# A network of six blocks on one core: context attention reordered, recurrent prologue with composite weights on four row groups

## The reference

```python
# block 1: cross attention, 16 heads of 8, padding mask over 512 keys
q = _ln((x @ Wq.T + bq).reshape(b, s1, h, d), qn_w, qn_b) * scale
k = _ln(k, kn_w, kn_b)
attn = jnp.where(padding_mask[:, None, None, :], einsum('bihd,bjhd->bhij', q, k), -inf)
ctx = einsum('bhij,bjhd->bihd', softmax(attn, axis=-1), v)
out = ctx @ Wo.T + bo
# blocks 2 and 3: self attention with a window, mixture of experts
# block 4: recurrent, 32 steps, with attention over the context in each
gates = concat([x_t, attn]) @ W_ih.T + b_ih + h @ W_hh.T + b_hh
i, f, g, o = split(gates, 4)
c = sigmoid(f) * c + sigmoid(i) * tanh(g);  h = sigmoid(o) * tanh(c)
attn = attend(h)
# block 5: four state space layers, in each
dt = (u @ xpw)[..., :DT_RANK]           # DT_RANK = 8
delta = softplus(dt @ dtw + dtb)
# block 6: experts with low-rank additions
```

## Time and profile before

| | us |
|---|---|
| median of 3 runs | 657.27 |
| lowest, highest run | 653.38, 658.79 |
| the profiled execution | 659.21 |
| its span (first to last instruction) | 657.1 |

### The profile page before, as it was taken

How to read it: one execution, slowest core, us unless ns; L and a number is a source line. 1 busy time by engine, 2 the same in 40 slices (tenths; PEclk the granted TensorE clock), 3 DMA queues, 4 the chain that set the end, 5 groups by cost and what they waited for, 6 DMA issues and landing times.

```text
span 657.1 us, 20737 instructions
## 1 busy us (share of the span) xinstructions
PE 557.8 (85%) x8469; PEld 426.5 (65%) x8469; DVE 470.8 (72%) x1829; ACT 311.0 (47%) x910; POOL 167.3 (25%) x209
## 2 busy tenths in 40 slices
PE   6968769769997999999999999966998898889847
PEld 4635545368875888888888888854655664666435
DVE  2867639865345777777777777752888998998882
ACT  2768729226556334444443444335545554554501
POOL 4245624127000000000000000005357346644700
PEclk9969979599995555555555555557988998999896
DMA  8900000010002000000000000000000000000000
GB/s 317 421 8 2 1 5 1 2 47 1 1 6 90 4 4 3 5 4 3 4 5 3 4 3 5 4 2 0 1 0 2 0 1 1 0 1 0 1 0 8
DMA packets 6255, 16.05 MB, mean 24 GB/s; under 512 B 2656, under 2 KB 3432, under 8 KB 5648
## 3 DMA queue, kind: packets, MB, share of 16 engines
q1 hardware_dynamic: 5744, 14.47, 6.0%
q10 hardware_dynamic: 416, 0.26, 0.1%
HBM read 14.60 MB, written 0.13 MB: 22 GB/s over the span
## 4 chain that ended last, share of the span: by engine, by line
PE 42%; DVE 31%; ACT 14%; issue 10%; POOL 2%; DMA 1%; DVEq 0%; ACTq 0%
PE bank L1715 7%; PE bank L1621 6%; PE bank L1783 6%; ACT esp L671 3%; PE bank L1551 3%; PE bank L1564 2%; DVE ssum L1164 2%; ACT a L658 2%; ACT e L673 2%; DVE w L1219 2%; DVE rz L1199 2%; DVE opre L1140 2%; DVE asp L1154 2%; DVE opre L1143 2%; DVE opre L1141 2%
## 5 line engine op out<-in xcount | busy, mean ns | idle before, releaser
L1621 PE MATMUL bank<-esp,qblk 128*128 128x1 f16 (+1 forms) x2048 | 66.6, 166 | 11.9 <-ACT esp L671 11.9
L1621 PEld LDWEIGHTS bank<-esp,qblk 128*128 128x128 f16 x2048 | 61.2, 104 | 17.3 <-ACT esp L671 17.3
L470 POOL MEMSET ctxT<- 128x128 f32 x1 | 0.3, 316 | 277.6 <-DVE xres L1206 277.6
L1621 PE MATMUL bank<-hsp,kT 128*128 128x2 f16 x2048 | 63.5, 166 | 2.0 <-DVE hsp L1192 1.9
L1621 PEld LDWEIGHTS bank<-hsp,kT 128*128 128x128 f16 x2048 | 59.5, 104 | 2.2 <-issue 2.2
L658 ACT ACTIVATE a<-opre 128x4 f32<-128x4 f32 x64 | 13.1, 205 | 80.6 <-DVE opre L1143 80.6
L1232 DVE SCALAR_TENSOR_TENSOR T<-bank,bct,T 128x256 f32<-128x256 f32 x112 | 46.4, 473 | 2.2 <-PE bank L1796 2.2
L1219 DVE TENSOR_TENSOR_SCAN qblk<-ctxT,bank 128x512 f32<-128x512 f32 x32 | 37.7, 1209 | 5.7 <-PE bank L1783 5.3
L665 ACT ACTIVATE gact<-bank,lgate 128x16 f32<-128x16 f32 x64 | 17.6, 275 | 46.4 <-PE bank L1621 46.4
L1219 DVE TENSOR_TENSOR_SCAN w<-kT,bank 128x512 f32<-128x512 f32 x32 | 37.6, 1206 | 1.1 <-PE bank L1783 1.1
L1783 PE MATMUL bank<-maskb,T 128*128 128x512 f32 x64 | 37.4, 712 | 0.5 <-ACT T L743 0.5
(11 more groups left out here) (326 smaller groups left out, 1403.7 us busy)
## 6 DMA issues: line engine op xcount, KB each, us to landing
w<-in_w_dram SPq DMA_DIRECT2D x2, 2048.0 KB
ctxT<-in_ctxT_dram SPq DMA_DIRECT2D x8, 256.0 KB, 6.2
wqkv<-in_qkvT_dram SPq DMA_DIRECT2D x1, 1536.0 KB, 12.1
w<-in_mw_dram SPq DMA_DIRECT2D x1, 1024.0 KB, 5.1
lw<-in_lw_dram SPq DMA_DIRECT2D x1, 960.0 KB, 25.0
rows<-in_rows_dram SPq DMA_DIRECT2D x1, 772.0 KB, 9.5
wqkv<-in_fw_dram SPq DMA_DIRECT2D x1, 532.0 KB, 3.5
T<-in_mask_dram SPq DMA_DIRECT2D x1, 512.0 KB, 6.0
```

Of the source, the lines that this page charges most:

```text
L1621: return pe.matmul(out, lhsT, rhs, start=start, stop=stop, skip_group_check=True)
```

## The change

In the context attention the instructions stay and their order changes on three engines. PE runs the scores one batch earlier, between the third and the fourth transpose of a batch, and each of the four now waits for one maximum; the values of a batch come after the transposes of the next. VectorE takes the reciprocal two groups behind the maximum and not one, and the copy and `x_heads` at other places. ScalarE runs up to five exponentials ahead of the copies.

In the recurrent prologue ScalarE writes only `gx32`; GpSimd makes the bfloat16 high part from it. The 8-row operands of the composite weights lie on four row groups (partitions 0, 32, 64 and 96), one for each layer, and the layers take turns. For this the transposes become matmuls with the identity, onto four groups of output partitions, with 32 columns of which 8 are meant; `dtw` is loaded by four DMAs; four copies to `xpd` take the place of two. ScalarE, not VectorE, copies the four products to `wdt`, after its table load. The semaphores `l_gxps` and `m_comp` become one, `l_ps`.

```diff
@@ -239,10 +239,10 @@
         m_out = lw[:, 0:ML * MC * D]
-        m_dt = maskb[:, :].bitcast(F32)[:, 0:ML * MC * MR]
+        m_dt = maskb[:, :].bitcast(F32)[:, 0:ML * MC * MR + 32]
         diagc = vx[:, :, :].rearrange("p n d -> p (n d)")
-        dtw = maskb[0:MR, :].bitcast(F32)[:, 1024:1024 + ML * MI]
-        xpd = wqkv[0:MR, 1856:1856 + ML * MI]
+        dtw = [maskb[32 * l:32 * l + MR, :].bitcast(F32)[:, 1024:1024 + MI] for l in range(ML)]
+        xpd = [wqkv[32 * l:32 * l + MR, 1856:1856 + MI] for l in range(ML)]
         biasT = sb("m_biasT", [2 * ML * MC, P])
@@ -287,11 +287,11 @@
              "f_gate", "f_sub", "f_exp", "f_cw", "f_cwps", "f_cwT", "f_h", "f_act", "f_y", "f_acc", "f_b2")
-        sems("d_lw", "l_w", "l_stat", "l_max", "l_scale", "l_kv", "l_hi", "l_rest", "l_gxps", "l_gx",
+        sems("d_lw", "l_w", "l_stat", "l_max", "l_scale", "l_kv", "l_hi", "l_rest", "l_ps", "l_gx", "l_gxhigh",
              "l_gxlow", "l_zero", "g_ps", "g_act", "c_new", "c_tanh", "h_hi", "h_lo", "s_hi", "m_c", "m_t", "m_d",
...
              "y_st", "y_tr")
-        sems("d_late", "d_ssm", "m_turns", "m_comp", "m_wdt", "m_setup",
+        sems("d_late", "d_ssm", "m_turns", "m_wdt", "m_setup",
              "m_xt", "m_xp", "m_uz", "m_up", "m_uc", "m_sig", "m_uu", "m_p", "m_bcs", "m_inv",
@@ -370,9 +370,10 @@
             sp.wait_ge(sem["x_res"], 1)
-            sp.dma_start(dtw, arr["dtw"]).then_inc(sem["d_ssm"], 16)
+            for l in range(ML):
+                sp.dma_start(dtw[l], arr["dtw"][:, l * MI:(l + 1) * MI]).then_inc(sem["d_ssm"], 16)
             m_proj = arr["mw"][:, ML * 2 * MI:ML * 2 * MI + ML * MC * (6 * MN + MR)].rearrange("p (n k) -> p n k", n=ML * MC)
-            sp.dma_start(m_dt.rearrange("p (n k) -> p n k", n=ML * MC), m_proj[:, :, 6 * MN:]).then_inc(sem["d_ssm"], 16)
+            sp.dma_start(m_dt[:, 0:ML * MC * MR].rearrange("p (n k) -> p n k", n=ML * MC), m_proj[:, :, 6 * MN:]).then_inc(sem["d_ssm"], 16)
@@ -380,7 +381,7 @@
             sp.dma_start(m_in, arr["mw"][:, 0:ML * 2 * MI]).then_inc(sem["d_late"], 16)
-            sp.wait_ge(sem["l_gxps"], 4)
+            sp.wait_ge(sem["l_ps"], 4)
             sp.dma_start(m_out, arr["mw"][:, ML * 2 * MI + ML * MC * (6 * MN + MR):]).then_inc(sem["d_late"], 16)
@@ -464,6 +465,10 @@
+            for g in range(4):
+                pool.wait_ge(sem["l_gx"], g + 1)
+                pool.tensor_scalar(gx[:, 0:S, 0, g, :], gx32[:, :, g * B:(g + 1) * B], 1.0, 0.0, ALU.mult, ALU.add) \
+                    .then_inc(sem["l_gxhigh"], 1)
             pool.wait_ge(sem["x_res"], 4)
@@ -542,11 +547,18 @@
-            for i in range((B + 1) * XG):
-                if i < B * XG:
-                    x_exp(i)
-                if i >= XG and i % XG != XG - 1:
-                    x_copy_pt(i - XG)
+            for i in range(XG + 1):
+                x_exp(i)
+            for i in range(0, B * XG, XG):
+                for k in range(2):
+                    x_copy_pt(i + k)
+                for k in (5, 6):
+                    if i + k < B * XG:
+                        x_exp(i + k)
+                x_copy_pt(i + 2)
+                for k in (7, 8):
+                    if i + k < B * XG:
+                        x_exp(i + k)
@@ -605,8 +617,8 @@
             act.wait_ge(sem["m_turns"], 1)
-            for k in range(2):
-                act.activation(xpd[:, k * 512:(k + 1) * 512], bank[2 + k][0:MR, :], ACT.Copy).then_inc(sem["m_wdt"], 1)
+            for l in range(ML):
+                act.activation(xpd[l], bank[2][32 * l:32 * l + MR, 0:MI], ACT.Copy).then_inc(sem["m_wdt"], 1)
             act.activation(biasT[:, :], bank[4][0:2 * ML * MC, 0:P], ACT.Copy).then_inc(sem["m_wdt"], 1)
@@ -642,13 +654,14 @@
             for g in range(4):
-                act.wait_ge(sem["l_gxps"], g + 1)
+                act.wait_ge(sem["l_ps"], g + 1)
                 share = bank[g][:, 0:TOK].rearrange("p (b t) -> p b t", b=B)
-                for to in (gx32[:, 0:1, g * B:(g + 1) * B], gx[:, 0:1, 0, g, :]):
-                    ins = act.activation(to_time(to), share, ACT.Identity, bias=gbias[:, g:g + 1],
-                                         scale=lgx[:, g // 3:g // 3 + 1])
-                ins.then_inc(sem["l_gx"], 1)
+                act.activation(to_time(gx32[:, 0:1, g * B:(g + 1) * B]), share, ACT.Identity, bias=gbias[:, g:g + 1],
+                               scale=lgx[:, g // 3:g // 3 + 1]).then_inc(sem["l_gx"], 1)
             act.preload_act_table_set("exp_and_others")
+            for l in range(ML):
+                act.wait_ge(sem["l_ps"], 4 + l + 1)
+                act.activation(wdt[l], bank[COMP[l]][:, :], ACT.Copy).then_inc(sem["m_wdt"], 1)
@@ -893,20 +906,18 @@
-            for b in range(B + 2):
-                for g in range(XG):
-                    i = b * XG + g
-                    if i < B * XG:
-                        x_max(i)
-                    if 1 <= i <= B * XG:
-                        x_norm(i - 1)
-                if b == 0:
+            for i in range((B + 3) * XG):
+                if i < B * XG:
+                    x_max(i)
+                if i % XG == XG - 1 and i >= 4 * XG - 1:
+                    x_heads(i // XG - 3)
+                if 2 <= i < B * XG + 2:
+                    x_norm(i - 2)
+                if i == 3:
                     step.sync()
                     dve.tensor_scalar(wmean[:, :], wmean[:, :], 1.0 / AD, None, ALU.mult).then_inc(sem["a_wmean"], 1)
-                if 1 <= b <= B:
-                    x_copy_pt(b * XG - 1)
-                if b >= 2:
-                    x_heads(b - 2)
+                if i % XG == 0 and 2 * XG <= i <= (B + 1) * XG:
+                    x_copy_pt(i - XG - 1)
@@ -1122,15 +1133,12 @@
             for g in range(4):
-                dve.wait_ge(sem["l_gx"], g + 1)
+                dve.wait_ge(sem["l_gxhigh"], g + 1)
                 whole, rest = (t[:, :, g * B:(g + 1) * B] for t in (gx32, gxrest))
...
                 dve.tensor_tensor(low, rest, mid, ALU.subtract).then_inc(sem["l_gxlow"], 1)
-                for l in ((), (0,), (1,), (2, 3))[g]:
-                    dve.wait_ge(sem["m_comp"], l + 1)
-                    dve.tensor_copy(wdt[l], bank[COMP[l]][:, :]).then_inc(sem["m_wdt"], 1)
@@ -1406,10 +1414,10 @@
                     pe.wait_ge(sem["k_hat"], B - 1)
-                else:
-                    pe.wait_ge(sem["x_max"], XG * b)
                 pe.wait_ge(sem["k_done"], b + 2)
                 for g in range(XG):
+                    if b:
+                        pe.wait_ge(sem["x_max"], XG * (b - 1) + g + 1)
                     own = slice(32 * g, 32 * g + 32)
@@ -1437,14 +1445,17 @@
-            for b in range(B + 2):
-                if b < B:
-                    x_scores(b)
-                if b >= 2:
-                    x_pv(b - 2)
-                if 1 <= b <= B:
-                    for g in range(XG):
-                        x_transpose((b - 1) * XG + g)
+            for b in range(2):
+                x_scores(b)
+            for b in range(B):
+                for g in range(XG - 1):
+                    x_transpose(b * XG + g)
+                if b < B - 2:
+                    x_scores(b + 2)
+                x_transpose(b * XG + XG - 1)
+                if b:
+                    x_pv(b - 1)
+            x_pv(B - 1)
             pe.wait_ge(sem["x_oT"], B + 1)
@@ -1527,9 +1538,11 @@
-            pe.wait_ge(sem["d_ssm"], 32)
-            for n in range(ML * MC):
-                pe.transpose(bank[2 + n // 4][0:MR, n % 4 * P:(n % 4 + 1) * P], m_dt[:, n * MR:(n + 1) * MR], ident)
+            pe.wait_ge(sem["d_ssm"], 16 * (ML + 1))
+            for l in range(ML):
+                for ch in range(MC):
+                    at = (l * MC + ch) * MR
+                    pe.matmul(bank[2][32 * l:32 * l + 32, ch * P:(ch + 1) * P], m_dt[:, at:at + 32], ident, start=True, stop=True)
             pe.transpose(bank[4][0:2 * ML * MC, 0:P], v("convb", 0, 2 * ML * MC), ident).then_inc(sem["m_turns"], 1)
@@ -1544,7 +1557,7 @@
                 if e == 1:
-                    pe.wait_ge(sem["m_wdt"], 3)
+                    pe.wait_ge(sem["m_wdt"], ML + 1)
                 w = w1[:, e * F:(e + 1) * F] if e < E else ws[:, 0:F]
@@ -1607,15 +1620,15 @@
                 pe.matmul(bank[g][:, 0:TOK], lw[:, g * D:(g + 1) * D], xnT[:, :], start=True, stop=True) \
-                  .then_inc(sem["l_gxps"], 1)
+                  .then_inc(sem["l_ps"], 1)
             pe.wait_ge(sem["l_rest"], 2 * B + 1)
-            for l in range(ML):
-                if COMP[l] == 1:
-                    pe.wait_ge(sem["l_gx"], 2)
-                for ch in range(MC):
-                    ins = pe.matmul(bank[COMP[l]][:, ch * MI:(ch + 1) * MI], xpd[:, l * MI + ch * P:l * MI + (ch + 1) * P],
-                                    dtw[:, l * MI:(l + 1) * MI], start=True, stop=True)
-                ins.then_inc(sem["m_comp"], 1)
+            pe.wait_ge(sem["l_gx"], 2)
```

(8 more changed lines are left out.)

## The result

The changed kernel takes 649.95 us (median of 4 runs, 649.26 to 650.93) beside 657.36 (653.38 to 658.79) of the kernel before: ratio 0.9896, 95% interval 0.9858 to 0.9935. That is 7.4 us less, inside the range of 643 to 654 and on the forecast side, 2.95 above the 647 that was named, and only just past the bound of one per cent. The profiled execution took 650.93, its span is 649.0, 8.1 less than before.

The account below looks back on a forecast made before the run. Attention was taken as bound by waits between engines (floor ScalarE's 4.40 us a batch), the prologue by PE's composite weights and VectorE's last split. Attention -7.5 and prologue -2.6 sum to -10.1: 647 us, range 643 to 654.

Parts of the forecast that it names:

- Head, -2.8 forecast: Context attention's start: scores waiting for single maxima bring maximum 8 to 44.8 instead of 47.64, -2.8 us.
- Clock, +0.9: Context attention: PE's full clock returns between 47 and 50, so most of the batch after 44.8 is PE-bound, +0.9 us.
- The rival by which it stays low: Context attention: PE stays at half clock, 3.05 us per batch, some 661.6 with all five; chance 0.15 for three to five.
- Middle, -4.5 (4.45 a batch): Context attention, five batches from maximum 8 to 28: 4.45 us each, 22.25 against 26.75, -4.5 us.
- this is tight, not late: Context attention's middle: transpose 4b+3 ends at 5.05, VectorE's copy of it stands at 5.07, so nothing is delayed.
- the waits only move: Rival: attention batches take 4.9 us (-2.2), prologue splits alternate with casts (-1.9), 650.2 us in all; chance 0.16.
- The price of a drain: Context attention: a fourth tiling-mode change per batch costs 0.2 us, making the whole gain 9.1, not 10.1; left out of the sum.
- Tail, -1.1: Context attention from maximum 28 to the residual: last heads start 9.25 behind maximum 28 instead of 10.36, -1.1 us.
- Prologue, -2.6 within -1.9 to -3.3: Recurrent prologue: recurrence starts between 207.4 and 208.8 instead of 210.75; -2.6 us taken.
- the alternation: Recurrent prologue: every GpSimd cast falls behind a group of VectorE subtractions, three more casts of 0.45 us, 208.8.
- that rival fell: Recurrent prologue: 8-row matmuls on row groups do not overlap, PE's 7.2 us stays, -7.5 alone, 649.8 us; chance 0.07.
- Parts at nothing: Dt-weight transposes as matmuls, four copies for two, three more DMA issues: idle time covers them, cost nothing.

Follow-up runs that it names:

- third experiment: Changed kernel with seven slots of `T` for the scores instead of six: 647.9 us, ratio 0.9843 to the kernel before.
- fourth experiments: Changed kernel with the scores of batch b+2 behind the fourth transpose of batch b: 649.18 us, ratio 0.9877 to the kernel before.
- first: Kernel before with only the new order of the context attention, recurrent prologue as before: 651.45 us, ratio 0.9930 to the kernel before.
- seventh: Changed kernel, but ScalarE writes the bfloat16 high part too and GpSimd casts nothing: 651.64 us, ratio 0.9932 to the kernel before.
- eighth experiments: Changed kernel with the composite weights' operands of all layers on partitions 0 to 7, one row group: 649.05 us, ratio 0.9907 to the kernel before.

## Why the prediction was right, and where a term was mis-sized

**The sum** was -10.1 and the two stages brought 8.4. The unchanged stages gave 0.1 between the two profiles (-1.9 - 1.1 + 2.9 + 0.2), by chance, and the start lost 0.2: 8.1 of span. The medians differ by 7.4. The sum came as close as it did partly by luck: the head, middle and tail fell 0.4, 1.5 and 1.2 short of their terms, and against them stood 0.9 that the clock was to cost the middle and did not, and 0.6 more in the recurrent block.

**Head, -2.8 forecast, -2.4 measured.** Maximum 8 is 11.69 and 10.28 behind maximum 0 in two profiles of the old order and 8.77 to 9.32 in four of the new one, so the head's gain is 1.0 to 2.9. The size holds within that; the reason does not. I gave it to the single waits on maxima, and with one wait for all maximum 8 stands at 9.1, where it stands with them. What helps must be the rest of the new order of PE and VectorE; no run takes it apart. And 1.9 to 2.5 more would have been had with the clock up.

**Clock, +0.9, measured nothing.** It was low in the head as assumed, though PE resumed at full clock and lost it 1.2 us later, and came back near 45 instead of 47 to 50: the batch that was to pay, from maximum 8 on, ran at 1.00 and took 3.89. The rival by which it stays low did not occur in any profile.

**Middle, -4.5 (4.45 a batch), measured 4.88 (-3.0 over the five batches).** This is the term that was mis-sized, and the step that failed is the sentence "this is tight, not late". I walked the batch along each engine with the durations of one, found three engines near 4.3 and let them fit. Two things were left out. Transpose 4b+2 can't follow 4b+1 at once but waits for ScalarE's copy of 4b. And the scores stand behind it: with t = 0 at maximum 4b+4 all four start at 3.8 and end at 5.1, where I had the fourth alone left at 3.6 and done 0.95 later, at 4.55; transpose 4b+3 ends at 5.7 and not at 5.05. PE's list of one batch with that round trip is 4.66 long, and 4.88 with the 0.22 for which the fourth score waits for a maximum; the seventh slot takes 0.22 off a steady batch, the scores behind the fourth transpose 0.25. The rival "the waits only move" had named 4.9; its case for the middle is the one that came true, though not its prologue. The price of a drain that the Trainium skill's rule suggested (TensorEngine Tiling (Array Packing), Tiling Modes, Key Properties) stays unseen: in the chain of waits the records follow one another across the changes of tile shape, 1.29, 0.59, 1.01, 0.60, without a gap of their own. As the ends of matmuls are modelled, a short one inside the records would not show.

**Tail, -1.1, measured +0.1.** VectorE's heads came 0.3 earlier and not 1.1: the last transposes end 8.1 behind maximum 28 and not 7.05, behind PE's round trips to ScalarE's copies, and the values of the last two batches both follow them, 1.95 us. And the bias met GpSimd's centring, 0.47 more, which the prediction did not look at: shortening a tail moves what runs beside it.

**Prologue, -2.6 within -1.9 to -3.3, measured -3.3.** The free end of the range, and -3.0 where the clock was low (11.5 behind the residual). Casts and subtractions do hold each other up, but by at most 0.21 a cast and 0.2 a subtraction, and no cast fell behind a whole group of subtractions. The row of 1.41 to 2.50, on which the alternation rested, was of a VectorE instruction 1.42 long; between instructions of 0.42 GpSimd gets through. The row groups did overlap at 8 rows, so that rival fell: 2.09 us at half clock (third experiment), against the 1.8 worked out.

**Parts at nothing.** They were. The composite weights' matmuls after the second attention, the four copies and the DMAs are in no chain of waits that was looked at, and ScalarE still idles 1.29 before the first gate activation, where 0.9 was worked out.

**The chances.** 0.74 for faster by over 1% was more than the numbers bore: the ratio's interval reaches to 0.9935. With a middle of 4.9 among the likeliest cases the sum is nearer 650, as that rival said, and 649.95 was measured.

## What to carry to other kernels

When several engines are each nearly full, don't take the busiest one as the period: write down the loop through each buffer and each in-order queue, with the round trips, and take the longest. Here two PSUM banks, six slots and PE's order made 4.88 where no engine had more than 4.4 to do. A new order pays when the instruction that frees a buffer stands ahead of the one that waits for something else: moving one copy by one place was worth 0.88 us a batch. Check a gain in the steady batches against the whole stage: two versions with shorter batches had stages no shorter, for their heads were longer. Look, too, at what the matmuls behind a pause of TensorE cost, and at which neighbour a shortened stage slides under.

## What the runs showed of the hardware

- Eight-row matmuls on four row groups and into four banks overlap: sixteen float32 records of 256 columns in 1.15 us at full clock and 2.09 at half. On one row group they took 4.10 at a mean clock of 0.89, though they wrote to four banks in turn all the same, and 7.19 at half clock, layer by layer.
- TensorE's granted clock fell to 0.50 (1.2 GHz) in a rest of 2.84 us (third and fourth experiments) or within 1.2 us behind it (the changed kernel, first, seventh and eighth experiments), with four matmuls of 32 rows ahead of the rest and four behind it. It stayed at 1.00 (2.4 GHz) when three full matmuls filled that rest.
- GpSimd and VectorE hold each other up in both ways: a VectorE instruction with one SBUF source took 0.94 under GpSimd's two-operand one and ended 0.2 us behind it, where it took 0.37 when it met only the last 0.2 us of it; a two-source subtraction took 0.62 and not 0.42 beside a GpSimd cast, and a cast up to 0.62 and not 0.41. The Trainium skill (GPSIMD Engine Reference, Key points) names VectorE's two-input instructions and its 2-port modes as those that contend; the trace agrees with it, and shows the wait on either side.
